# One more state's drive product on GpSimd, in one unit of a selective scan

## The chip, the cores and the metric

The kernel runs on one core of a Trainium2 chip. The metric is the device time of one execution in microseconds (us), as the median of several runs. TensorE does matrix products, VectorE elementwise work and the scans, ScalarE activations, GpSimd elementwise work on SBUF alone and the scatters, SyncE issues DMAs.

## The reference, cut to what matters

One layer: a Mamba block (selective scan) with residual, then a mixture of eight experts, on x of shape 4 x 32 x 32 x 64, that is four batches of 1024 tokens. In the block 128 channels carry 16 states each:

```
def step(h, inp):
    u_t, d_t, B_t, C_t = inp
    dA = exp(d_t[..., None] * A)
    h = dA * h + (d_t * u_t)[..., None] * B_t[:, None, :]
    y = einsum('bdn,bn->bd', h, C_t)
```

For each state n the kernel therefore needs a decay, exp(delta * A[n]), a drive, (delta * u) * B[n], the scan over the tokens, and the product of h with C[n], which is summed over the states.

## The kernel before, in words

Channels lie on the 128 partitions and tokens along the free dimension, so one state of one batch is a tile of 128 x 1024. The work is cut into five units: three whole batches (units 0, 1 and 2), the first 768 tokens of the fourth (unit 3, CARRY) and its last 256 (unit 4, LAST). Every engine has its program written out by hand; the engines meet only through semaphores, and each takes its instructions in program order. For units 0 to 3 each engine loops over n = 0..15.

For one state n of unit v, with k = 16 v + n:

- SyncE loads row n of B into the tile bsb (L398) and of C into csb (L405), each broadcast over the partitions, in rings of four. The load of a B row waits until the drive four states back is counted in s_mul, that of a C row until the product four states back is counted in s_pP. Both are in one queue, in the order C(n), B(n+2).
- ScalarE writes the decay to dA (L697, `decay`), a ring of three, two states ahead.
- VectorE multiplies delta * u, which lies in the PSUM tile Cp, by the row of B into the PSUM tile Bp (L1277, `drive`), and then scans dA and Bp into h (L1318, `scan`). The drive of the next state follows each scan, since Bp holds one state.
- GpSimd multiplies h by the row of C into prod (L518, `scan` of that engine), and TensorE adds prod to Yp (L984).

A state in the list POOLED goes another way. GpSimd makes its drive in place in bsb (L567, `drive` of that engine) from te, the SBUF copy of delta * u, two states ahead in its loop. VectorE skips L1277 for it. Since Bp is then free, ScalarE writes the decay of that state into Bp (L707, `decay_pooled`), in two halves of 512 tokens: the first once the first half of the scan of state n-1 has been made, the second once that scan is whole. So the scans of n-1 and of n are both cut in two (SPLIT), and each half scan of n waits for its half of the decay. The list holds states 2 and 5 of units 1, 2 and 3. The counts s_dA and s_mul of a pooled state are added with those of the next state.

Beside its states each unit's loop carries the `front` of the next batch (projections, delta, delta * u) and the `back` of the unit before (norms, routing, rows for the scatter), piece by piece: front(f, n) and back(v, n) are the pieces with number n. ScalarE's loop for one n is, in this order:

```
if n + 2 < 16 and (v, n + 2) not in POOLED:
    decay(v, n + 2)
if (v, n + 1) in POOLED:
    decay_pooled(v, n + 1)
```

then back (for n under 8) and front(v+1, n). Its front has at n = 4 two table loads around the silus, at n = 5 and 6 the two halves of what delta is made of (L665 and L666, each half behind a "step" matmul L963 on TensorE), at n = 6 also the exponential of it (L669), and at n = 7 its logarithm (L672, L674). TensorE's loop at n = 6 has the 8 product pairs L1024 of back, which wait for ScalarE's copy bT (L748), ahead of L963. GpSimd's front has at n = 7 a sum that waits for that exponential (L526), and at 9, 12 and 13 three more products; VectorE's front has at n = 11 a COPY_PREDICATED (L1270; batch 0 has its own at L1440), and its back has at n = 8 the residual add L1343.

After the units come the routed rows: scatters to a table in DRAM (L558), the expert stage on TensorE (L1142, L1153, L1167) and the scatter of the result.

Of the kernel before, what the change touches and what calls it, by code (L numbers as in the profile page):

```python
# [38 lines left out]
LAST, CARRY = V - 1, V - 2  # L39
NOWHERE = 1 << 20  # L40
CSLOTS = 4
POOLED = [(v, n) for v in range(1, LAST) for n in (2, 5)]
SPLIT = [(v, n + i) for v, n in POOLED for i in (-1, 0)]


# [17 lines left out]
def metaformer_layer(nc, x, ln_g, ln_b, in_proj_w, conv_w, conv_b, x_proj_w, dt_proj_w, dt_proj_b, A_log,  # L63
# [7 lines left out]
    with ExitStack() as ctx:  # L71
# [179 lines left out]
        def at(buf, b):  # L251

            return buf[:, b % 2, :]
# [112 lines left out]
        def _(sp):  # L366
# [52 lines left out]
            for v in range(LAST):  # L419
# [3 lines left out]
                for n in range(N):  # L423
# [9 lines left out]
                    if v == CARRY and n == 7:  # L433
                        sp.wait_ge(p_bx, len(POOLED))
                    if v == CARRY and n == 4:
# [23 lines left out]
        def _(pool):  # L459
# [60 lines left out]
            def front(f, n):  # L520
                if n == 9:
                    pool.wait_ge(f_ln, f + 1)
                    po.tensor_tensor(tabs[:, :], yt_free[:, :], tabs[:, :], ALU.subtract).then_inc(f_less, 1)
                if n == 7:
                    pool.wait_ge(f_exp, f + 2)
                    po.tensor_tensor(trel[:, :], trel[:, :], ex[:, :], ALU.add).then_inc(f_high, 1)  # L526
                if n == 12:
                    pool.wait_ge(f_pick, f + 1)
                    pool.wait_ge(f_high, f + 1)
                    if f >= 2:  # L530
                        pool.wait_ge(s_dA, N * (f - 1))
                    po.tensor_tensor(at(delta, f), trel[:, :], tabs[:, :], ALU.subtract).then_inc(f_delta, 1)
                if n == 13:
                    pool.wait_ge(f_delta, f + 1)
                    po.tensor_tensor(te[:, :], at(delta, f), at(u, f), ALU.mult).then_inc(f_dus, 1)
# [26 lines left out]
            def drive(v, n):  # L562
                k, c = N * v + n, span(v)
                pool.wait_ge(f_dus, UNITS[v][0])
                pool.wait_ge(b_in[k % CSLOTS], 16 * (k // CSLOTS + 1))
                row = bsb[:, k % CSLOTS, c]
                po.tensor_tensor(row, te[:, c], row, ALU.mult).then_inc(p_bx, 1)  # L567

            last_slot = po.to_reg(E * CAP - 1)
            for v in range(LAST):  # L570
                for n in range(16):
# [4 lines left out]
                    if v + 1 < B:  # L576
                        front(v + 1, n)
                    if (v, n + 2) in POOLED:
                        drive(v, n + 2)
# [43 lines left out]
        def _(act):  # L623
# [5 lines left out]
            def front(f, n):  # L629
# [45 lines left out]
                if n == 8:  # L675
                    ac.activation(yt_free[:, :], yt_free[:, :], ACT.Copy, bias=-1.0).then_inc(f_ln, 1)
                    act.wait_ge(p_bx, sum(x < f for x, _ in POOLED))
                    ac.activation(te[:, :], ex[:, :], ACT.Square, scale=0.5 ** 0.5)
# [14 lines left out]
            def decay(v, n):  # L693
                k, c = N * v + n, span(v)
                if k >= 3:
                    act.wait_ge(s_scan, k - 2)
                ac.activation(dA[:, k % 3, c], at(delta, UNITS[v][0])[:, c], ACT.Exp,  # L697
                              scale=aneg[:, n:n + 1]).then_inc(s_dA, 2 if (v, n - 1) in POOLED else 1)

# [135 lines left out]
            for v in range(LAST):  # L835
# [5 lines left out]
                for n in range(16):  # L841
                    if n + 2 < 16 and (v, n + 2) not in POOLED:
                        decay(v, n + 2)
# [717 lines left out]
```

## Time and profile before

| | us |
|---|---|
| median of 3 runs | 388.14 |
| lowest and highest run | 387.02, 391.14 |
| span of the profiled execution | 397.8 |
| VectorE busy in it | 310.1 (78%) |
| TensorE busy | 316.1 (79%) |
| GpSimd busy | 282.1 (71%) |
| ScalarE busy | 233.3 (59%) |

The span goes from the first instruction to the last one of one execution under the profiler. The page gives no other time of that execution; the runs are timed without it. Busy shares are averages over stages with different limits. Unit 1 lies at about 100 to 162 us.

### The profile page before, as it was taken

The numbers are of one execution on the slowest core, as the hardware profiler recorded it, in microseconds if no ns is written. First come the engines' busy times: TensorE is split into PE (matmuls) and PEld (weight loads), VectorE is DVE, ScalarE is ACT, GpSimd is POOL, SyncE is SP. The second block draws the span as 40 slices with busy tenths as digits, with TensorE's granted clock in tenths as the row PEclk, the third lists the DMA queues.
The fourth block names the chain that finished last, engine by engine and source line by source line (L and its number), as shares of the span: only waits on it lengthen the run. The fifth ranks groups of instructions, "written<-read, shape, count | busy, mean of one in ns | idle before, by whom it ended". The sixth has DMA issues, their size and how long they took to land. (4 is left out here: it accounts for less than half of the span.)

```text
span 397.8 us, 4347 instructions
## 1 busy us (share of the span) xinstructions
PE 316.1 (79%) x1257; PEld 188.4 (47%) x1257; DVE 310.1 (78%) x360; ACT 233.3 (59%) x519; POOL 282.1 (71%) x201
## 2 busy tenths in 40 slices
PE   7832986957989896897989698796895798869784
PEld 3311432313535352553545265363773576748764
DVE  4799987999999999987999989999981157425441
ACT  4456797524798984659797268775651455234221
POOL 3435846987993999999599999966877044745760
PEclk9965897999998998879899898989987599968955
DMA  4287999999798699856878769997210900000000
GB/s 99 36 281 248 274 243 366 390 200 368 315 315 323 208 308 297 284 190 244 303 254 298 203 175 325 318 369 226 61 30 19 250 23 4 18 8 17 16 1 8
DMA packets 43986, 78.68 MB, mean 198 GB/s; under 512 B 16050, under 2 KB 26093, under 8 KB 43962
## 3 DMA queue, kind: packets, MB, share of 16 engines
q1 hardware_dynamic: 41066, 73.88, 57.5%
q0 software_dynamic: 2896, 4.53, 4.2%
q8 instruction: 10, 0.16, 0.2%
q14 instruction: 14, 0.11, 0.1%
HBM read 72.30 MB, written 7.54 MB: 201 GB/s over the span
## 5 line engine op out<-in xcount | busy, mean ns | idle before, releaser
L518 POOL TENSOR_TENSOR prod<-h,csb 128x1024 f32<-128x1024 f32 (+1 forms) x64 | 143.7, 2253 | 24.9 <-DMA csb<-bc_rows 10.5
L984 PE MATMUL Yp<-prod,ident 128*128 128x512 f32 (+1 forms) x256 | 124.9, 624 | 13.8 <-POOL prod L518 13.6
L1318 DVE TENSOR_TENSOR_SCAN h<-dA,Bp 128x1024 f32<-128x1024 f32 (+2 forms) x58 | 119.7, 2064 | 4.7 <-DVE Bp L1277 1.0
L984 PEld LDWEIGHTS Yp<-prod,ident 128*128 128x128 f32 x256 | 50.3, 208 | 75.3 <-issue 50.3
L697 ACT ACTIVATE dA<-delta,aneg 128x1024 f32<-128x1024 f32 (+1 forms) x58 | 62.9, 1093 | 23.1 <-DVE h L1318 19.0
L1277 DVE TENSOR_TENSOR Bp<-Cp,bsb 128x1024 f32<-128x1024 f32 (+1 forms) x58 | 67.7, 1168 | 6.4 <-DMA bsb<-bc_rows 4.2
L615 POOL DMA_INDIRECT out_dram<-dA,csb x30 | 30.3, 1009 | 36.5 <-DVE dA L1509 28.9
L558 POOL DMA_INDIRECT slots<-rows_,slot x30 | 30.1, 1002 | 6.9 <-issue 4.5
L1495 DVE TENSOR_TENSOR dA<-Bp,b2s 128x320 f32<-128x320 f32 (+1 forms) x8 | 3.8, 475 | 33.8 <-PE Bp L1167 15.6
L1153 PE MATMUL Cp<-prod,w1s 128*128 128x384 f32 (+1 forms) x64 | 24.7, 508 | 2.0 <-issue 2.0
L895 ACT ACTIVATE bsb<-Yp,b1c 128x256 f32<-128x256 f32 x16 | 7.6, 475 | 23.4 <-PE Yp L1184 14.0
L1167 PEld LDWEIGHTS Bp<-w2s,prod 128*128 128x128 f32 x152 | 18.5, 195 | 2.3 <-issue 1.0
L1167 PE MATMUL Bp<-w2s,prod 128*128 128x64 f32 x152 | 18.3, 276 | 0.2 <-ACT prod L888 0.2
L1196 PEld LDWEIGHTS M<-w2s,bsb 128*128 128x128 f32 x64 | 13.6, 269 | 7.3 <-issue 5.7
L1196 PE MATMUL M<-w2s,bsb 128*128 128x64 f32 x64 | 12.9, 344 | 4.8 <-issue 4.8
L1153 PEld LDWEIGHTS Cp<-prod,w1s 128*128 128x128 f32 x64 | 12.1, 216 | 7.4 <-issue 5.4
L878 ACT ACTIVATE prod<-Bp 64x384 f32<-64x384 f32 (+1 forms) x16 | 6.8, 427 | 14.8 <-PE Bp L1142 7.6
L1184 PE MATMUL Yp<-hxT,w1s 72*128 72x256 f32 x32 | 13.7, 519 | 0.6 <-issue 0.6
L567 POOL TENSOR_TENSOR bsb<-te,bsb 128x1024 f32<-128x1024 f32 (+1 forms) x6 | 13.1, 2179 | 1.2 <-DMA bsb<-bc_rows 1.1
L615 POOL DMA_INDIRECT out_dram<-dA,bsb x10 | 10.1, 1013 | 4.7 <-issue 2.9
L526 POOL TENSOR_TENSOR trel<-trel,ex 128x1024 f32<-128x1024 f32 x3 | 7.1, 2359 | 8.7 <-DVE h L1318 4.9
L886 ACT ACTIVATE prod<-Cp,b1c 128x384 f32<-128x384 f32 (+1 forms) x16 | 8.4, 525 | 7.9 <-PE Cp L1153 5.8
(290 smaller groups left out, 604.8 us busy)
## 6 DMA issues: line engine op xcount, KB each, us to landing
bsb<-bc_rows SPq DMA_DIRECT2D x48, 512.0 KB, 6.7
csb<-bc_rows SPq DMA_DIRECT2D x48, 512.0 KB
bsb<-bc_rows SPq DMA_DIRECT2D x16, 384.0 KB, 5.7
csb<-bc_rows SPq DMA_DIRECT2D x16, 384.0 KB
slots<-fill POOLq DMA_DIRECT2D x1, 2600.0 KB
csb<-slots SPq DMA_DIRECT2D x6, 325.0 KB, 5.3
bcs<-bc_rows SPq DMA_DIRECT2D x2, 512.0 KB, 10.9
xs_in<-in_x_dram SPq DMA_DIRECT2D x1, 768.0 KB, 5.8
```

The costliest lines, as they stand in the source:

```text
L518: po.tensor_tensor(prod[:, k % 4, c], h[:, k % 3, c], csb[:, k % CSLOTS, c], ALU.mult).then_inc(s_pP, 1)
L558: po.indirect_dma_start(slots_dram[:, :], bass.IndirectOffsetOnAxis(ap=slot[:, v % 2, t:t + 1], axis=0), rows(v)[:, t, :], None, bounds_ch ...
L567: po.tensor_tensor(row, te[:, c], row, ALU.mult).then_inc(p_bx, 1)
L615: po.indirect_dma_start(out_rows, bass.IndirectOffsetOnAxis(ap=xe[e][:, k, R_ID:R_ID + 1].bitcast(I32), axis=0), yo[:, e % 2, k, :], None, ...
L697: ac.activation(dA[:, k % 3, c], at(delta, UNITS[v][0])[:, c], ACT.Exp, scale=aneg[:, n:n + 1]).then_inc(s_dA, 2 if (v, n - 1) in POOLED e ...
L984: ins = te_.matmul(Yp[:, c], idn, prod[:, k % 4, c], start=False, stop=(n == 15), skip_group_check=True)
L1153: te_.matmul(Cp[:, k * HALF:k * HALF + (k1 - k0) * P], w1s[:, e, k * P:(k + 1) * P], xT[:, e % 2, k0 * P:k1 * P], start=True, stop=True).t ...
L1167: ins = te_.matmul(turned_down(i)[:, (k - k0) * C:(k - k0 + 1) * C], part[:, e % 2, k * P:(k + 1) * P], w2s[:, e, x, :], start=(x == 0), s ...
L1184: te_.matmul(Yp[:, j % 2 * HALF:j % 2 * HALF + LW], w1s[0:HX, e, part * P:(part + 1) * P], hxT[0:HX, :], start=True, stop=True).then_inc(d ...
L1196: ins = te_.matmul(M0[:, t * C:(t + 1) * C], hid[:, j % 2, t * P:(t + 1) * P], w2s[:, e, part, :], start=False, stop=(j == BLOCKS - 1 and ...
L1277: ve.tensor_tensor(Bp[:, span(v)], Cp[:, span(v)], bsb[:, k % CSLOTS, span(v)], ALU.mult).then_inc(s_mul, 2 if (v, n - 1) in POOLED else 1)
L1318: ins = ve.tensor_tensor_scan(h[:, k % 3, c], decays, drives, h[:, k % 3, c.start - 1:c.start] if i else 0.0, ALU.mult, ALU.add)
```

## The change

State 8 of unit 1 joins the list POOLED. Its drive is then made by GpSimd ahead of its product of state 6, its decay goes to Bp in two halves, and the scans of states 7 and 8 of unit 1 are cut in two. Everything else follows from the list: in unit 1 the decay of state 8 is no longer issued at n = 6 of ScalarE's loop, its two halves are issued at n = 7, behind the decay of state 9, and VectorE's drive of state 9 counts for two.

```
-POOLED = [(v, n) for v in range(1, LAST) for n in (2, 5)]
+POOLED = [(v, n) for v in range(1, LAST) for n in ((2, 5, 8) if v == 1 else (2, 5))]
 SPLIT = [(v, n + i) for v, n in POOLED for i in (-1, 0)]
```

## Rows read from the trace of the kernel before

**Rows 1.** The page: its first line, and one line of its DMA issues.

```profile
span 397.8 us, 4347 instructions
...
bsb<-bc_rows SPq DMA_DIRECT2D x48, 512.0 KB, 6.7
```

**Rows 2.** The chain that ended last, its first piece kept: start, length, what.

```profile
280.11 1.30 DVE h L1297 x2
```

**Rows 3.** Busy time in stretches: start:end length, each engine, clock, DMA.

```profile
125.00:165.00 40.00, 33.65 (x114) 15.97 (x112) 38.84 (x37) 28.75 (x58) 35.88 (x17) 0.96 0.86 286
...
230.00:280.00 50.00, 40.91 (x193) 26.02 (x192) 46.29 (x53) 35.27 (x109) 40.92 (x31) 0.93 0.86 280
```

**Rows 4.** Timeline of VectorE, unit 2, the scan of state 5.

```profile
181.22 1.22 DVE L1318 TENSOR_TENSOR_SCAN h<-Bp,bsb 128x512 f32<-128x512 f32 x1 [3.37 <-ACT Bp L707]
...
183.93 1.23 DVE L1277 TENSOR_TENSOR Bp<-Cp,bsb 128x1024 f32<-128x1024 f32 x1
```

**Rows 5.** Timeline of VectorE, unit 1, states 4 to 9: start, length, instruction.

```profile
112.15 1.22 DVE L1318 TENSOR_TENSOR_SCAN h<-dA,Bp 128x512 f32<-128x512 f32 x1
...
114.60 1.20 DVE L1318 TENSOR_TENSOR_SCAN h<-Bp,bsb 128x512 f32<-128x512 f32 x1
...
118.60 2.29 DVE L1318 TENSOR_TENSOR_SCAN h<-dA,Bp 128x1024 f32<-128x1024 f32 x1
...
122.25 2.29 DVE L1318 TENSOR_TENSOR_SCAN h<-dA,Bp 128x1024 f32<-128x1024 f32 x1
124.56 1.23 DVE L1277 TENSOR_TENSOR Bp<-Cp,bsb 128x1024 f32<-128x1024 f32 x1
125.89 2.29 DVE L1318 TENSOR_TENSOR_SCAN h<-dA,Bp 128x1024 f32<-128x1024 f32 x1
128.21 1.23 DVE L1277 TENSOR_TENSOR Bp<-Cp,bsb 128x1024 f32<-128x1024 f32 x1
```

**Rows 6.** Timeline of TensorE ahead of the second half of front(2,6).

```profile
122.92 1.90 PE L1024 MATMUL M<-PW,bT 65*128 65x64 f32 x16
124.65 1.08 PE L963 MATMUL M<-u,wdt 128*128 128x512 f32 x2
```

**Rows 7.** Timeline of ScalarE, unit 1; in brackets the idle time before, and its end.

```profile
121.80 0.57 ACT L748 ACTIVATE bT<-M 65x512 f32<-65x512 f32 x1
...
123.42 1.14 ACT L697 ACTIVATE dA<-delta,aneg 128x1024 f32<-128x1024 f32 x1
125.76 0.69 ACT L665 ACTIVATE tabs<-M,dtb 128x512 f32<-128x512 f32 x1 [1.20 <-PE M L963]
...
128.07 1.13 ACT L697 ACTIVATE dA<-delta,aneg 128x1024 f32<-128x1024 f32 x1
```

**Rows 8.** Timeline of ScalarE, unit 2, before the half decays of state 5.

```profile
174.10 0.22 ACT L733 ACTIVATE sq<-M 128x64 f32<-128x64 f32 x1 [4.54 <-PE M L1006]
...
179.38 1.14 ACT L697 ACTIVATE dA<-delta,aneg 128x1024 f32<-128x1024 f32 x1
180.42 1.29 ACT L707 ACTIVATE Bp<-delta,aneg 128x512 f32<-128x512 f32 x2
```

**Rows 9.** Timeline of GpSimd, unit 1, products 5 and 6 and front at n = 7.

```profile
117.32 2.36 POOL L518 TENSOR_TENSOR prod<-h,csb 128x1024 f32<-128x1024 f32 x1 [0.15 <-DVE h L1318]
121.02 2.36 POOL L518 TENSOR_TENSOR prod<-h,csb 128x1024 f32<-128x1024 f32 x1 [1.34 <-issue]
128.24 2.37 POOL L526 TENSOR_TENSOR trel<-trel,ex 128x1024 f32<-128x1024 f32 x1 [4.86 <-DVE h L1318]
```

**Rows 10.** Timeline of SyncE's queue, the load of B's row 8 of unit 1.

```profile
112.09 0.32 SPq L398 DMA_DIRECT2D bsb<-bc_rows  x1
```

**Rows 11.** Timeline of VectorE, the two predicated copies, batch 0's and unit 1's.

```profile
26.33 1.29 DVE L1440 COPY_PREDICATED tabs<-small,te 128x1024 f32<-128x1024 uint8 x1
...
140.68 2.68 DVE L1270 COPY_PREDICATED tabs<-small,te 128x1024 f32<-128x1024 uint8 x1
```

**Rows 12.** Busy time in one stretch of unit 2; columns as in the third group.

```profile
168.00:170.00 2.00, 2.00 (x6) 1.31 (x6) 1.89 (x2) 1.55 (x2) 2.00 (x1) 0.50 0.69 263
```

## What the change should do to the time

> **What bounds the kernel now.** I read four views, in this order. The page gives the span of the profiled execution, 397.8 us [rows 1]. The chain that ended last is kept only from 280.11 us on [rows 2]; it begins with a VectorE scan of the last unit and goes on through TensorE's expert stage, so it says where the end hangs on VectorE, and nothing of the stretch that is changed. For that I cut the span into stretches: in 125 to 165 us VectorE is busy 38.84 of 40.00 us, against 35.88 on GpSimd and 28.75 on ScalarE; in 230 to 280 it is 46.29 of 50.00 [rows 3]. The gaps that are left there are mostly the 0.1 us between dependent instructions. So from the second batch's unit (unit 1, about 100 to 162 us) to the chain's first piece, VectorE's own order of instructions sets the time, and what it loses or wins in unit 1 arrives at the end unless a later wait takes it up. The only longer wait is one of 3.37 us in unit 2 for ScalarE's half decay, L707 [rows 4]. It is of the very kind that the change makes a third of, so its cause counts.
>
> The last view is the timeline of each engine over states 4 to 9 of unit 1. The reader is to see in it that an idle engine (GpSimd before L526) has room, and that a ScalarE that shows busy and waiting pieces in turn still decides when its next piece can come, since it takes its work in program order.
>
> **What the change takes from VectorE.** State 8's product (L1277, 1.23 us) goes, and the scans of states 7 and 8 are cut in two halves each, as those of states 4 and 5 are now. An uncut pair with both products goes from the scan of state 6 at 118.60 to that of state 8 at 125.89, 7.29 us; the cut pair from 112.15 to 118.60, 6.45 us [rows 5]. If nothing is late the change saves 7.29 - 6.45 = 0.84 us.
>
> **What it asks of ScalarE.** State 8's decay is no longer written to dA ahead of time. It goes into the PSUM tile Bp in two halves, the first after the first half scan of state 7. In ScalarE's order it stands elsewhere too: decay(8) was issued at n=6, before front(2,6); the two halves come at n=7, behind front(2,6) and decay(9). Front(2,6) can't start early. It waits for the second "step" matmul L963, which TensorE runs at 124.65 for 1.08 us, behind L1024 (122.92, 1.90 us) [rows 6]; L1024 itself waits for the copy bT at 121.80 [rows 7]. ScalarE gets to front(2,6) at 125.76 after 1.20 us of idling; without decay(8) (123.42, 1.14 us) it idles longer and starts at the same 125.76. decay(9) starts at 128.07 [rows 7], and its own condition, the end of scan 6, was met at 120.89. These times don't move, so the working is:
> - decay(9) at 128.07. From a decay to the half decay behind it is 180.42 - 179.38 = 1.04 us in unit 2 [rows 8]: first half at 129.11.
> - From there to the half scan that waits for it is 181.22 - 180.42 = 0.80 us [rows 4, 8]: state 8's scan starts at 129.91. VectorE has finished state 7 at 122.25 + 2.45 = 124.70 (two half scans take 2.45 us from 112.15 to the next at 114.60 [rows 5]). That is a stall of 5.2 us, and nothing else is in VectorE's order between the two.
> - From that half scan to the next product is 183.93 - 181.22 = 2.71 us [rows 4]: the product of state 9 starts at 132.62, against 128.21 now [rows 5]. The lateness is **4.4 us** (5.2 of stall less 0.84 saved, within rounding).
>
> Behind the wait VectorE has the residual add L1343 and then everything else of unit 1, which is its dense stretch. ScalarE's own later work slips far less: front(2,7) stands behind the two halves, which take 1.29 us together in unit 2 [rows 8], and VectorE, later by 4.4, doesn't wait for it.
>
> Bounds of this term: if L1024 starts as soon as the bT copy ends (121.80 + 0.57 = 122.37 instead of 122.92), all comes 0.55 us earlier, 3.9 us; if L963 ran at half clock, its 1.08 us doubled, 5.5 us. I take 4.4, the value of the rows themselves.
>
> **What it asks of GpSimd and the queues.** GpSimd gets one more product before product 6. Two of its instructions set end to end are 2.3 to 2.4 us apart, so it would run from about 119.7 to 122.0, behind product 5 (117.32, 2.36), and product 6 moves from 121.02 to 122.0, 1 us. The cover is the 4.86 us that GpSimd waits before L526 at 128.24 [rows 9], a wait that the row puts down to a scan long done; by the code it ends with front(2,6)'s exponential, done just before decay(9), and so stays. With product 6 done by 124.4 all is as before: cost nothing. Without that cover it would be 2.4 us on GpSimd, and VectorE would see them only after the two states by which a scan may run ahead of products. The new product needs row 8 of B, issued at 112.09 [rows 10]; a load takes 6.7 us to land [rows 1], so 118.8 and a little, just in time. Its result is wanted only at 129.9: 7.9 us to spare.
>
> On SyncE's queue the row of state 12 waits for the product of state 9, since that increment now stands for two: 132.6 + 1.23 = 133.9. Behind it stand the C rows of 11 and later. Product 7 sets the first of these (near 132.9, as now), so C row 11 is issued about 134.3, lands near 141, and is wanted by product 11 at about 144, since scans are later by 4.4. B row 12 lands near 141 too, its product comes near 144. Cost nothing, with some 3 us to spare.
>
> COPY_PREDICATED in unit 1 (L1270) meets GpSimd in another phase. It takes 2.68 us there and 1.29 at the start, where GpSimd stands still [rows 11]. Ends: 1.29 (-1.4 us) and 1.29 behind a whole product of 2.36, 3.65 (+1.0); I take no change, since a product lies beside it in both kernels. The Trainium skill's page "SBUF — State Buffer", section "Who interferes with whom", says that a VectorE instruction with two SBUF inputs and a GpSimd one that reads SBUF block each other for a whole instruction; the trace agrees, 2.68 against 1.29. By that rule the copy, which I work out to begin about 1.1 us into product 11, would wait out the other 1.25 and take 2.5 in all, and the sum would be 4.3 in place of 4.4.
>
> A scan isn't stretched by GpSimd's products: that at 125.89, with GpSimd idle, is followed by its next product after 2.32 us, that at 122.25, partly under product 6, after 2.31 [rows 5, 9]. Were scan 6 held by the new product after all, by 2.4 us at most, state 7's scan would still end before the half decay is written: nothing.
>
> **The sum.** 4.4 us on the way to the end of unit 1. Unit 2's start is a chain that VectorE sets off (yt, TensorE's projection, ScalarE's squares after a wait of 4.54 us, then the half decays [rows 8]), so it moves along. Units 2 and 3 are dense, and the expert stage follows the last rows. 397.8 [rows 1] becomes 402.2 in a profile. The timed median, 388.14, is 9.7 us under the span; I take that gap as untouched and add the same 4.4 us to the median: 392.5, 1.1% slower. A measurement of this kernel can tell about 1% (3.9 us) from no change, since its three runs lie 4.1 us apart.
>
> **Rivals.**
> - *The change does what it says*: the half decay is there when VectorE wants it, and 0.84 us are saved: 387.3. It decides by whether ScalarE writes the first half by 124.7. It speaks for it that five of the six cut pairs now go through without such a wait. Against it: in those the half decay doesn't stand behind a wait for TensorE, and here it would have to come 5.2 us earlier than the order allows. 0.06.
> - *The loss is given back in unit 2.* The 3.37 us stall there came with TensorE at a granted clock of 0.50, that is at 1.2 GHz, in all of 168 to 170 us [rows 12], inside the chain that leads to it. If the later schedule leaves it at 2.4 GHz there, the stall goes and 4.4 - 3.4 = 1.0 remains: 389.2. For it: TensorE's work and pauses ahead of it are moved. Against: they come in the same order. 0.20.
> - *More than the sum*: TensorE, which waits longer in unit 1, meets the half clock where ScalarE hangs on it, in L1024 and L963 (twice 1.90 and 1.08 is 3.0 us more at most) or at the start of unit 3, where the pair at state 5 has no room either. 4.4 + 1.1 to 4.4 + 3.0: 393.6 to 395.5. 0.14.
>
> **How the numbers follow.** My forecast has 0.60: 392.5, by its bounds 391.5 to 393.6. The range takes in the second rival and most of the third, and leaves out the first and the far end of the third, about 0.12, and some for the spread of the medians: 389.0 to 394.6. The bound for slower, 392.0, lies just under my forecast: of its 0.60 I put 0.41 above, with the third rival's 0.14 that is 0.55. Faster by over 1% is in none of the cases by itself; 0.02 for spread. Within 1%: the remaining 0.43.
>
> **What would show it.** In the changed profile: a wait of about 5 us of VectorE before state 8's first half scan, ended by ScalarE L707; ScalarE's two halves right behind decay(9); GpSimd's seven L567 with the new one near 120 us and its wait before L526 still there, shorter at its start; COPY_PREDICATED between 1.3 and 3.7 us; unit 2's stall again near 3.4. I am wrong if that wait is under 2 us, if the half decays stand before front(2,6), or if unit 2's stall is gone.

## The result, and the profile after

The changed kernel is slower. Its first four runs have a median of 394.99 us (391.56 to 399.54), four runs of the kernel before beside them one of 387.58 (384.58 to 391.14); the ratio is 1.0158, 95% interval 1.0098 to 1.0218, that is 3.8 to 8.5 us. A second measurement, six runs against 23, gave 392.69 and 1.0181 (1.0123 to 1.0238).

VectorE's timeline in unit 1 of the changed kernel, against [rows 5]; in brackets the idle time before, and its end:

```profile
118.80 2.29 DVE L1318 TENSOR_TENSOR_SCAN h<-dA,Bp 128x1024 f32<-128x1024 f32 x1
...
122.44 1.22 DVE L1318 TENSOR_TENSOR_SCAN h<-dA,Bp 128x512 f32<-128x512 f32 x1
123.69 1.28 DVE L1318 TENSOR_TENSOR_SCAN h<-dA,h,Bp 128x512 f32<-128x512 f32 x1
130.10 1.22 DVE L1318 TENSOR_TENSOR_SCAN h<-Bp,bsb 128x512 f32<-128x512 f32 x1 [5.13 <-ACT Bp L707]
...
132.81 1.23 DVE L1277 TENSOR_TENSOR Bp<-Cp,bsb 128x1024 f32<-128x1024 f32 x1
```

State 8's first half scan waits 5.13 us for ScalarE's half decay. From the scan of state 6 to the product of state 9 it is 132.81 - 118.80 = 14.01 us, against 128.21 - 118.60 = 9.61 before: 4.40 us lost. ScalarE's timeline shows why, against [rows 7]:

```profile
125.95 0.69 ACT L665 ACTIVATE tabs<-M,dtb 128x512 f32<-128x512 f32 x1 [2.24 <-PE M L963]
...
128.26 1.13 ACT L697 ACTIVATE dA<-delta,aneg 128x1024 f32<-128x1024 f32 x1
129.30 1.28 ACT L707 ACTIVATE Bp<-delta,aneg 128x512 f32<-128x512 f32 x2
```

Without decay(8) in its way ScalarE idles 2.24 us where it idled 1.20, and gets to front(2,6) no earlier, 7.15 us behind the start of scan 6 against 7.16. The half decays follow it and decay(9).

GpSimd's timeline, against [rows 9]: the new product runs from 120.03, product 6 comes 1.1 us later against product 5 than before, and 3.74 of the 4.86 us of waiting before L526 are left.

```profile
117.52 2.36 POOL L518 TENSOR_TENSOR prod<-h,csb 128x1024 f32<-128x1024 f32 x1 [0.16 <-issue]
120.03 2.35 POOL L567 TENSOR_TENSOR bsb<-te,bsb 128x1024 f32<-128x1024 f32 x1 [0.16 <-DMA bsb<-bc_rows]
122.34 2.35 POOL L518 TENSOR_TENSOR prod<-h,csb 128x1024 f32<-128x1024 f32 x1
128.43 2.35 POOL L526 TENSOR_TENSOR trel<-trel,ex 128x1024 f32<-128x1024 f32 x1 [3.74 <-ACT ex L669]
```

Further on, VectorE of the changed kernel at four points of units 2 to 4, and then the same of the kernel before but for the first, which is in [rows 4]:

```profile
182.35 1.20 DVE L1318 TENSOR_TENSOR_SCAN h<-Bp,bsb 128x512 f32<-128x512 f32 x1
...
208.43 5.17 DVE L1270 COPY_PREDICATED tabs<-small,te 128x1024 f32<-128x1024 uint8 x1
...
234.81 1.23 DVE L1333 TENSOR_TENSOR yt<-Yp,sz 128x1024 f32<-128x1024 f32 x1 [1.63 <-PE Yp L984]
...
281.10 1.23 DVE L1284 TENSOR_TENSOR Bp<-Cp,trel 128x1024 f32<-128x1024 f32 x1
```

```profile
207.33 3.13 DVE L1270 COPY_PREDICATED tabs<-small,te 128x1024 f32<-128x1024 uint8 x1
...
230.55 1.23 DVE L1333 TENSOR_TENSOR yt<-Yp,sz 128x1024 f32<-128x1024 f32 x1 [0.51 <-PE Yp L984]
...
276.55 1.23 DVE L1284 TENSOR_TENSOR Bp<-Cp,trel 128x1024 f32<-128x1024 f32 x1
```

The stall of 3.37 us at state 5 of unit 2 [rows 4] is gone here. TensorE's granted clock (the last number but two of these rows) was 1.00, that is 2.4 GHz, in the chain ahead of it at 170 to 176 us, where the kernel before had 0.53, mostly 1.2 GHz, at 166 to 172:

```profile
170.00:176.00 6.00, 6.00 (x37) 4.50 (x37) 5.77 (x5) 3.90 (x13) 5.02 (x4) 1.00 0.54 184
```

```profile
166.00:172.00 6.00, 6.00 (x24) 4.81 (x23) 5.68 (x6) 2.71 (x4) 5.17 (x5) 0.53 0.47 159
```

But the gain didn't last. COPY_PREDICATED of unit 2 took 5.17 us where it took 3.13, and yt (L1333) at the start of unit 3 waited 1.63 us for TensorE where it waited 0.51. At the first product of unit 4 the lateness is 281.10 - 276.55 = 4.55 us, 4.35 without the 0.20 by which unit 1 had begun later. The second profile of the changed kernel shows the same three: 5.13, 5.14 and 1.49 us.

**The clock between runs.** Nearly every run has its mean granted TensorE clock on record, and the time goes with it: the kernel before ran from 384.51 us at 0.897 to 391.47 at 0.864 in that second group. At 0.905 to 0.906 the kernel before took 386.34 to 386.62 us there (five runs), the changed one 391.23 (one run); at 0.869 it is 391.32 against 395.43 and 396.26. The distance at a like clock is thus 4 to 5 us. A line through the 176 runs of this study that have a clock on record, with one slope for the clock and one offset for each kernel, has 1.53 us for each 0.01, and these offsets from the kernel before (95%, in us; the scatter around the line is 1.4; the kernels are described in the next section):

| kernel | runs | ratio to the runs beside it | offset at a like clock |
|---|---|---|---|
| changed kernel | 10 | 1.0158, 1.0181 | +5.4 ± 0.9 |
| product of state 8 on VectorE | 6 | 1.0179 (1.0122 to 1.0236) | +4.5 ± 1.2 |
| copy apart from products | 10 | 1.0053 (1.0011 to 1.0095) | +3.2 ± 1.0 |
| early half decays | 12 | 1.0085 (1.0045 to 1.0125) | +1.7 ± 0.9 |
| extra GpSimd product alone | 12 | 1.0066 (1.0029 to 1.0104) | +0.7 ± 0.9 |
| two units | 12 | 1.0017 (0.9967 to 1.0067) | -0.9 ± 0.9 |
| early, product 7 first | 12 | 0.9970 (0.9915 to 1.0024) | -1.0 ± 0.9 |
| all cures | 12 | 0.9987 (0.9944 to 1.0029) | -1.3 ± 0.9 |
| GpSimd's cures without state 8 | 12 | 0.9977 (0.9929 to 1.0026) | -1.7 ± 0.9 |

The ratios go by the runs within 1.5% of the fastest of their kernel, the medians and the line by all runs; a line through the former alone puts the offsets up to 0.9 us elsewhere, the extra product's at +1.4 ± 0.9. The offsets describe; a kernel may also change how often the clock falls, and that part is then not in its offset.

### The profile page after: what moved, and what is told of

It is laid out like the page before. It is cut to its first block and busy times, and to the rows that moved or that the text cites. A ratio compares the mean times of both kernels' runs of the same rounds, so it can differ in the third digit from the quotient of the medians.

```text
span 392.4 us, 4352 instructions
## 1 busy us (share of the span) xinstructions
PE 306.9 (78%) x1257; PEld 181.5 (46%) x1257; DVE 310.8 (79%) x361; ACT 233.9 (60%) x520; POOL 282.2 (72%) x202
## 5 line engine op out<-in xcount | busy, mean ns | idle before, releaser
L518 POOL TENSOR_TENSOR prod<-h,csb 128x1024 f32<-128x1024 f32 (+1 forms) x64 | 141.9, 2221 | 32.3 <-DVE h L1318 11.6
L984 PE MATMUL Yp<-prod,ident 128*128 128x512 f32 (+1 forms) x256 | 129.4, 645 | 12.5 <-POOL prod L518 12.5
L1318 DVE TENSOR_TENSOR_SCAN h<-dA,Bp 128x1024 f32<-128x1024 f32 (+2 forms) x57 | 116.4, 2041 | 5.0 <-DVE Bp L1277 1.7
L984 PEld LDWEIGHTS Yp<-prod,ident 128*128 128x128 f32 x256 | 52.0, 214 | 74.7 <-issue 53.1
L1153 PE MATMUL Cp<-prod,w1s 128*128 128x384 f32 (+1 forms) x64 | 21.6, 462 | 0.0
L567 POOL TENSOR_TENSOR bsb<-te,bsb 128x1024 f32<-128x1024 f32 (+1 forms) x7 | 15.4, 2207 | 0.3 <-DMA bsb<-bc_rows 0.2
L707 ACT ACTIVATE Bp<-delta,aneg 128x512 f32<-128x512 f32 (+1 forms) x14 | 9.1, 657 | 7.9 <-DVE h L1318 7.6
L1318 DVE TENSOR_TENSOR_SCAN h<-Bp,bsb 128x512 f32<-128x512 f32 x7 | 8.5, 1209 | 5.3 <-ACT Bp L707 5.1
L1208 PE MATMUL Yp<-h,ident 128*128 128x256 f32 x32 | 10.1, 464 | 1.9 <-POOL h L591 1.9
L691 ACT ACTIVATE Cp<-te 128x1024 f32<-128x1024 f32 x3 | 3.1, 1029 | 14.0 <-DVE Bp L1277 14.0
```

What stands on the lines that cost most here:

```text
L518: po.tensor_tensor(prod[:, k % 4, c], h[:, k % 3, c], csb[:, k % CSLOTS, c], ALU.mult).then_inc(s_pP, 1)
L707: ac.activation(Bp[:, c], at(delta, UNITS[v][0])[:, c], ACT.Exp, scale=aneg[:, n:n + 1]).then_inc(p_dA, 1)
L984: ins = te_.matmul(Yp[:, c], idn, prod[:, k % 4, c], start=False, stop=(n == 15), skip_group_check=True)
L1153: te_.matmul(Cp[:, k * HALF:k * HALF + (k1 - k0) * P], w1s[:, e, k * P:(k + 1) * P], xT[:, e % 2, k0 * P:k1 * P], start=True, stop=True).t ...
L1208: ins = te_.matmul(Yp[:, c], idn, h[:, ring(p // 2), (p % 2 * 2 + i) * LW:(p % 2 * 2 + i + 1) * LW], start=False, stop=(p == 7 and i == 1) ...
L1318: ins = ve.tensor_tensor_scan(h[:, k % 3, c], decays, drives, h[:, k % 3, c.start - 1:c.start] if i else 0.0, ALU.mult, ALU.add)
```

## The experiments

**Early half decays.** The changed kernel with this in ScalarE's loop, for (1, 8) alone:

```
+EARLY = [(1, 8)]
...
-                    if n + 2 < 16 and (v, n + 2) not in POOLED:
+                    if n + 2 < 16 and (v, n + 2) not in POOLED and (v, n + 1) not in EARLY:
                         decay(v, n + 2)
-                    if (v, n + 1) in POOLED:
+                    if (v, n + 1) in POOLED and (v, n + 1) not in EARLY:
                         decay_pooled(v, n + 1)
+                    if (v, n + 2) in EARLY:
+                        decay_pooled(v, n + 2)
+                        decay(v, n + 3)
```

> The changed kernel, but in unit 1 ScalarE issues the two half decays of state 8, and then decay(9), at n=6 ahead of front(2,6) instead of behind it; GpSimd's third product, the cut scans and all else stay. Theory (the place of the half decays in ScalarE's order): VectorE's wait of 5.13 us before state 8's scan falls under 0.3 us, the product of state 9 starts 0.8 us earlier than in the kernel before, front(2,6) starts about 0.8 us later; the time is that of the kernel before, ratio 0.985 to 1.005. Rival (GpSimd's added product, or its use of SBUF beside VectorE, costs the time): it is still made, so the ratio stays at 1.010 to 1.020. Rival (cutting the scans costs more than it saves): the product of state 9 starts later than before though there is no wait.

Ratio 1.0085 (1.0045 to 1.0125), offset +1.7 us: most of the loss is gone, not all, and the ratio is over the 1.005 expected. VectorE's timeline (the file's lines lie four further down, so L1322 is the scan and L1281 the product):

```profile
123.59 1.28 DVE L1322 TENSOR_TENSOR_SCAN h<-dA,h,Bp 128x512 f32<-128x512 f32 x1
124.78 1.20 DVE L1322 TENSOR_TENSOR_SCAN h<-Bp,bsb 128x512 f32<-128x512 f32 x1
...
127.46 1.23 DVE L1281 TENSOR_TENSOR Bp<-Cp,bsb 128x1024 f32<-128x1024 f32 x1
...
131.51 1.23 DVE L1281 TENSOR_TENSOR Bp<-Cp,bsb 128x1024 f32<-128x1024 f32 x1
133.74 2.29 DVE L1322 TENSOR_TENSOR_SCAN h<-dA,Bp 128x1024 f32<-128x1024 f32 x1 [0.99 <-POOL prod L519]
```

State 8 no longer waits, as expected. But the scan of state 10 waits 0.99 us for GpSimd's product 7, and that stands behind L526 (here L527) in GpSimd's order:

```profile
122.36 2.35 POOL L519 TENSOR_TENSOR prod<-h,csb 128x1024 f32<-128x1024 f32 x1
129.03 2.36 POOL L527 TENSOR_TENSOR trel<-trel,ex 128x1024 f32<-128x1024 f32 x1 [4.32 <-ACT ex L670]
131.35 4.69 POOL L519 TENSOR_TENSOR prod<-h,csb 128x1024 f32<-128x1024 f32 x2
```

So a second wait lay hidden behind the first: GpSimd idles 4.32 us for an exponential, with the scan for product 7 already made.

**The changed kernel again**, without an edit, as the yardstick.

> The changed kernel itself again, as the yardstick of this group. Theory: 4.4 us, ratio 1.011; with the first measurement's 1.0158 in the interval. VectorE waits about 5.1 us before state 8's first half scan in this profile too, whatever the end of the kernel does. If the excess over 4.4 us is real and not scatter, the ratio comes out at 1.015 or more with an interval that leaves out 1.011.

1.0181, with 1.011 just outside; at a like clock +5.4 us, one more than my 4.4. The wait is 5.13 us again.

**The product of state 8 on VectorE.** GpSimd makes two products in unit 1, ScalarE's order is the changed one:

```
-                    if (v, n + 2) in POOLED:
+                    if (v, n + 2) in POOLED and (v, n + 2) != (1, 8):
                         drive(v, n + 2)
...
+                if (v, n + 1) == (1, 8):
+                    k = N * v + n + 1
+                    dve.wait_ge(b_in[k % CSLOTS], 16 * (k // CSLOTS + 1))
+                    row = bsb[:, k % CSLOTS, span(v)]
+                    ve.tensor_tensor(row, Cp[:, span(v)], row, ALU.mult).then_inc(p_bx, 1)
```

> The changed kernel, but VectorE makes the drive of state 8 itself, in place in bsb, behind the cut scan of state 7; GpSimd makes two products in unit 1 as before. The half decays stay behind front(2,6). Theory (ScalarE's order): VectorE does the 1.2 us product inside its wait, which shrinks from 5.1 to about 3.8 us and ends at the same point; the product of state 9 starts where it does in the changed kernel, and the time is the changed kernel's, ratio 1.008 to 1.018. Rival (GpSimd's added product costs the time): the product is gone, so the ratio falls to 0.995 to 1.005.

Ratio 1.0179, as slow as the changed kernel. Its timeline of VectorE:

```profile
125.04 1.20 DVE L1327 TENSOR_TENSOR bsb<-Cp,bsb 128x1024 f32<-128x1024 f32 x1
130.25 1.22 DVE L1318 TENSOR_TENSOR_SCAN h<-Bp,bsb 128x512 f32<-128x512 f32 x1 [4.01 <-ACT Bp L707]
```

The product that the change took off VectorE fits into VectorE's wait, which shrinks to 4.01 us and ends where it did. Whether GpSimd or VectorE makes it doesn't matter while ScalarE is late.

**The extra GpSimd product alone**, in the kernel before:

```
+                    if (v, n) == (1, 6):
+                        po.tensor_tensor(extra[:, :], te[:, :], te[:, :], ALU.mult).then_inc(x_done, 1)
                     scan(v, n)
```

with a wait of ScalarE for x_done before it writes te again.

> The kernel before with one more GpSimd product of the same size at the same place (te times te into a tile that nothing reads, ahead of product 6 of unit 1); state 8 keeps VectorE's product and the decay in dA. Theory: product 6 starts 1 us later, GpSimd's wait before L526 shrinks from 4.9 to 3.7 us, VectorE shows no new wait, ratio 0.995 to 1.005. Rival (GpSimd's added product costs the time): ratio 1.006 to 1.020, and VectorE's scans or products beside it last longer or wait for GpSimd.

By its ratio, 1.0066, it missed: the interval leaves out no change. At a like clock the offset is +0.7 ± 0.9 us. Its one run at 0.905 took 386.39 us, where five of the kernel before took 386.34 to 386.62; six of its twelve runs lay under a clock of 0.875, and six of the 23 beside it. So the ratio is at least in part a matter of which clock its runs met; whether the extra product has a part in that, or a cost of its own, stays open. In the profile no scan or product of VectorE in states 6 to 9 waits, and GpSimd still waits 4.39 us before L526 (here L528). The extra product was shorter than the true one, 1.89 us:

```profile
121.86 1.89 POOL L583 TENSOR_TENSOR extra<-te 128x1024 f32<-128x1024 f32 x1
...
130.47 2.37 POOL L528 TENSOR_TENSOR trel<-trel,ex 128x1024 f32<-128x1024 f32 x1 [4.39 <-DVE h L1324]
```

**Half the dose.** The changed kernel with the half decays of state 8 ahead of decay(9), still behind front(2,6):

```
+                    if (v, n + 1) == (1, 8):
+                        decay_pooled(v, n + 1)
                     if n + 2 < 16 and (v, n + 2) not in POOLED:
                         decay(v, n + 2)
-                    if (v, n + 1) in POOLED:
+                    if (v, n + 1) in POOLED and (v, n + 1) != (1, 8):
                         decay_pooled(v, n + 1)
```

> The changed kernel, but ScalarE issues the two half decays of state 8 ahead of decay(9) and still behind front(2,6). A half dose: theory says that the first half starts where decay(9) did, 1.04 us earlier, so VectorE's wait falls from 5.13 to about 4.1 us and the product of state 9 starts 1.0 us earlier. A theory that puts the wait down to GpSimd's product or to its row of B expects no change of the wait.

```profile
129.25 1.22 DVE L1320 TENSOR_TENSOR_SCAN h<-Bp,bsb 128x512 f32<-128x512 f32 x1 [4.09 <-ACT Bp L707]
```

4.09 us: one decay less ahead of the halves, 1.04 us less of wait. It ran once (392.68 us), so its time says little.

**Product 7 first.** Early half decays, and in GpSimd's loop for n = 7 of unit 1:

```
-                    if v + 1 < B:
+                    if v + 1 < B and (v, n) != (1, 7):
                         front(v + 1, n)
                     if (v, n + 2) in POOLED:
                         drive(v, n + 2)
                     scan(v, n)
+                    if (v, n) == (1, 7):
+                        front(v + 1, n)
```

> The kernel with the early half decays, and in unit 1 GpSimd makes product 7 ahead of front(2,7) (L526) instead of behind it. Theory (with ScalarE on time, GpSimd's order is next in line): VectorE's wait of 0.99 us for product 7, before the scan of state 10, is gone, GpSimd's wait before L526 shrinks by about 2.3 us, and from unit 1's first product to the scan of state 10 VectorE is 0.8 us ahead of the kernel before. Ratio 0.992 to 1.006; among runs of like granted clock within 1 us of the kernel before. Rival (GpSimd has no room at all in this unit): the wait only moves to a later scan of unit 1 and stays near 1 us.

Ratio 0.9970 (0.9915 to 1.0024), offset -1.0 us; no scan of unit 1 behind state 8 waits for a product. GpSimd makes product 7 at 127.49 us now, and VectorE's scan of state 10 follows without a wait:

```profile
127.49 2.36 POOL L519 TENSOR_TENSOR prod<-h,csb 128x1024 f32<-128x1024 f32 x1 [0.62 <-issue]
```

```profile
135.32 2.29 DVE L1324 TENSOR_TENSOR_SCAN h<-dA,Bp 128x1024 f32<-128x1024 f32 x1
```

In this profile a stall of 3.18 us at state 5, ahead of all this, had put VectorE later against GpSimd; the kernel with all cures, whose unit 1 had no stall, shows the same without it.

**The copy apart from products.** The changed kernel, with GpSimd waiting for COPY_PREDICATED one state sooner:

```
+                if n == 11:
+                    pool.wait_ge(f_pick, f + 1)
                 if n == 12:
                     pool.wait_ge(f_pick, f + 1)
```

> The changed kernel, but GpSimd waits for COPY_PREDICATED (L1270) ahead of product 11 instead of behind it, in every unit. Theory (the copy is held up by GpSimd's products, and back to back products can take the shared way twice): the copy never meets two products, so its 5.17 us of unit 2 fall to 3.65 or less; unit 1's 2.5 us stay between 1.3 and 3.7. VectorE's wait of 5.1 us before state 8's scan stays. Ratio 1.008 to 1.018, at most 2 us under the changed kernel. Rival (the 5.17 us have nothing to do with GpSimd, but come from the copy's inputs): the copy of unit 2 still takes about 5 us where VectorE reaches it early.

```profile
149.05 1.30 DVE L1272 COPY_PREDICATED tabs<-small,te 128x1024 f32<-128x1024 uint8 x1
...
211.03 2.84 DVE L1272 COPY_PREDICATED tabs<-small,te 128x1024 f32<-128x1024 uint8 x1
```

1.30 us with GpSimd waiting beside it, as at the start [rows 11], and 2.84 behind a product. Ratio 1.0053 (expected 1.008 to 1.018), offset +3.2 us, 2.2 under the changed kernel (2.0 at most expected), with VectorE's wait at state 8 still there (5.54 us).

**All cures**: the last two edits and the early half decays together.

> Both cures together: early half decays, product 7 ahead of L526, and GpSimd waiting for COPY_PREDICATED ahead of product 11. Theory: VectorE has no wait in unit 1, the copies take 1.3 to 2.6 us where they took 2.7 to 3.3, and the time is 0.5 to 2.5 us under the kernel before at a like granted clock; ratio 0.990 to 1.003. Rival (GpSimd becomes late by waiting): VectorE's scans of states 13 to 15 wait for products, and the time is over that of the kernel before.

VectorE's timeline of unit 1 (L1326 is the scan, L1285 the product, L1278 the copy):

```profile
118.32 2.29 DVE L1326 TENSOR_TENSOR_SCAN h<-dA,Bp 128x1024 f32<-128x1024 f32 x1
...
124.42 1.20 DVE L1326 TENSOR_TENSOR_SCAN h<-Bp,bsb 128x512 f32<-128x512 f32 x1
...
127.10 1.23 DVE L1285 TENSOR_TENSOR Bp<-Cp,bsb 128x1024 f32<-128x1024 f32 x1
...
132.47 2.29 DVE L1326 TENSOR_TENSOR_SCAN h<-dA,Bp 128x1024 f32<-128x1024 f32 x1
...
139.57 1.99 DVE L1278 COPY_PREDICATED tabs<-small,te 128x1024 f32<-128x1024 uint8 x1
```

Nothing waits from state 6 to the copy. From the scan of state 6 to the product of state 9 it is 8.78 us, against 9.61 in [rows 5]: 0.83 saved. The copies took 1.99 us here and 2.79 in unit 2, the latter over the 2.6 expected. The time is 386.46 against 388.37 beside it, ratio 0.9987, offset -1.3 us.

**GpSimd's cures without state 8**: product 7 first and the copy apart, in the kernel before.

> The kernel before with GpSimd's two changes of order alone: product 7 of unit 1 ahead of L526, and the wait for COPY_PREDICATED ahead of product 11; two products per unit as before. It tells what of the time of the kernel with all cures is owed to the third state. Theory: the copies cost 0.5 to 1.5 us less in all, so the time is 0.5 to 1.5 us under the kernel before at a like clock, ratio 0.994 to 1.002, and the kernel with the third state on top is 0.8 us under this one. Rival (the third state is worth nothing even when nothing is late): this kernel is as fast as that one.

Offset -1.7 us, ratio 0.9977. It isn't slower than the kernel with all cures; 0.84 us between the two is less than these runs tell: they ran in different groups, on different chips, and with an offset for each group as well the line has -1.6 ± 1.0 for all cures and -1.1 ± 1.0 without state 8. That the third state pays in the time is thus not shown.

**Two units**: all cures, with state 8 pooled, its half decays early and product 7 first in unit 2 as well.

> The kernel with all cures, and state 8 pooled in unit 2 as well, with its half decays ahead of front(3,6) and product 7 ahead of L526 there too. Theory: no wait of VectorE before state 8 of unit 2, another 0.84 us saved there, ratio 0.990 to 1.001, 0.8 us under the kernel with one unit at a like clock. Rival (GpSimd, which also issues eight scatters in unit 2, has no room): VectorE waits for products in unit 2, and the time is 1 to 4 us over that kernel.

Offset -0.9 us: no gain from the second unit. VectorE, GpSimd and ScalarE in unit 2, one line of each:

```profile
190.79 1.22 DVE L1326 TENSOR_TENSOR_SCAN h<-Bp,bsb 128x512 f32<-128x512 f32 x1 [0.76 <-ACT Bp L712]
```

```profile
188.34 2.36 POOL L570 TENSOR_TENSOR bsb<-te,bsb 128x1024 f32<-128x1024 f32 x1
```

```profile
188.75 0.69 ACT L712 ACTIVATE Bp<-delta,aneg 128x512 f32<-128x512 f32 x1 [0.33 <-DVE h L1326]
```

The profile puts the 0.76 us down to ScalarE, whose first half had been done at 188.75 + 0.69 = 189.44. GpSimd's product ended at 190.70, and that is what the scan waited for: in unit 2 GpSimd also issues a scatter of 1.01 us in each of these states. The wait takes back nearly all of the 0.84 us. The rival for that unit was right in its mechanism, not in its price: it had 1 to 4 us over the kernel with all cures, and the offsets lie 0.4 us apart.

## Why the prediction was right, and where not

- **ScalarE's order** was the cause, and its working held to a tenth: a wait of 5.13 us for 5.2, a loss of 4.40 for 4.4. Moving the half decays ahead of front(2,6) took the wait away, moving them by one decay took 1.04 us of it, and taking the product off GpSimd again took nothing.
- **0.84 us saved** when nothing is late: 0.83 in the kernel with all cures. The rows show it; it is under what the times tell.
- **GpSimd's product at nothing** held in the rows: 3.74 us of cover were left in the changed kernel and 4.32 with the half decays early. In the times the extra product alone is +0.7 ± 0.9, which doesn't exclude a small cost. The 0.99 us that VectorE waited for product 7 with ScalarE on time, two states later as I had named, isn't the added product's: GpSimd idled 4.32 us ahead of L526, and product 7 stands behind that. In the kernel before, product 7 (the first of two in this row) was done at about 132.9 us, and the scan of state 10 began at 133.58:

```profile
130.56 4.70 POOL L518 TENSOR_TENSOR prod<-h,csb 128x1024 f32<-128x1024 f32 x2
```

```profile
133.58 2.29 DVE L1318 TENSOR_TENSOR_SCAN h<-dA,Bp 128x1024 f32<-128x1024 f32 x1
```

  That is 0.7 us of room. With the half decays early VectorE comes 0.8 us sooner and the exponential 0.7 us later, so the room is gone.
- **SyncE's queue** did as worked out: B row 12 was issued at 134.07 (133.9 forecast), C row 11 at 134.44 (134.3), and no one waited for either.

```profile
134.07 0.32 SPq L398 DMA_DIRECT2D bsb<-bc_rows  x1
134.44 0.43 SPq L405 DMA_DIRECT2D csb<-bc_rows  x1
```

- **COPY_PREDICATED** took 2.48 us in unit 1, 2.51 in the second profile:

```profile
145.29 2.48 DVE L1270 COPY_PREDICATED tabs<-small,te 128x1024 f32<-128x1024 uint8 x1
```

  The rule of the Trainium skill, page "SBUF — State Buffer", section "Who interferes with whom", that the later of two such instructions is blocked for the whole of the other, had given 2.5; the trace agrees in unit 1. In unit 2 the copy would by that rule have taken 3.0 us had it had the next turn, an estimate from the rows (1.67 us left of a product, then 1.29); it took 5.17, held up by two products. The step of the prediction that failed is the upper bound, "1.29 behind a whole product", and that I asked for it in unit 1 alone.
- **Unit 2's stall**, the second rival: it went, in both profiles of the changed kernel, and I had named that as a sign of being wrong. It stayed in those with the product on VectorE, 3.35, and with half the dose, 3.39. These came to unit 2 as late as the changed kernel (yt at 168.78 and 168.44 us against 168.69), but their granted clock was 0.50 in 174 to 176 us, where the changed kernel had 1.00. So the mechanism of the rival is there, but being late isn't enough for it, and what kept the clock up stays open. Its result isn't there: 4.40 - 3.37 + 2.04 (copy) + 1.12 (yt) = 4.2 us, against 4.35 measured. In this part the sum came out by luck: a gain of 3.37 us that the forecast didn't have was made up by 3.16 us of losses that it didn't have either. I had left out who would be met by a VectorE that comes early there.
- **The gap of 9.7 us** between span and median was misread. The changed kernel's profiled execution took 394.15 us with a span of 392.4, so 1.8 us lie around a span. The profile of the kernel before caught an execution with a long last stage; this row of it, in the expert stage, is far behind the change:

```profile
355.63 0.49 DVE L1495 TENSOR_TENSOR dA<-Bp,b2s 128x320 f32<-128x320 f32 x1 [10.84 <-remote]
```

  It did no harm, since I added a difference, but "402.2 in a profile" came out as 392.4.
- **The size.** 4.4 us lie inside 3.8 to 8.5; at a like clock it is 5.4 ± 0.9, a little more. The copy is a likely place, since keeping it apart from the products took 2.2 us off the changed kernel; how often it meets two products in runs without a profile wasn't seen, and so this stays argued. The end of the units is another. Here is yt of unit 4, first in the changed kernel, then in the kernel before:

```profile
308.25 0.42 DVE L1333 TENSOR_TENSOR yt<-Yp,sz 128x256 f32<-128x256 f32 x1 [2.98 <-PE Yp L1208]
```

```profile
302.08 0.42 DVE L1333 TENSOR_TENSOR yt<-Yp,sz 128x256 f32<-128x256 f32 x1 [2.98 <-PE Yp L1208]
```

  Less the 0.20 the lateness is 5.97 us there, where it was 4.35 at the first product of unit 4; in the second profile of the changed kernel yt comes at 305.68, 3.9 us late by the same count. So from one execution to the next the loss differs by 2 us before the expert stage begins.

## What to carry to other kernels

An instruction that is moved from "long ahead" to "just in time" has to be followed in the order of the engine that issues it: what stands in front of it there, and what that in turn waits for, is its price. When a wait of 5 us goes, look for the next one in the other engines' orders before counting the gain: here one cure in ScalarE's order needed another in GpSimd's. And where one kernel's runs differ by more than the effect, compare them at a like granted clock, or count from the rows of a stretch.

## What the runs showed of the hardware that was not expected

The predicated copy, with two inputs in SBUF, took 1.3 us with GpSimd still, 2 to 3.4 us beside one of its products, and twice 5.1 to 5.2 us. In that case three products of GpSimd ran back to back:

```profile
205.46 6.96 POOL L518 TENSOR_TENSOR prod<-h,csb 128x1024 f32<-128x1024 f32 x3
213.68 2.41 POOL L532 TENSOR_TENSOR delta<-trel,tabs 128x1024 f32<-128x1024 f32 x1 [1.25 <-DVE tabs L1270]
```

VectorE's copy was in line from 208.43, during the second product; the third began behind it at about 210.1 and yet ran first, to 212.4, and the copy took the 1.2 us from there to 213.6, in which GpSimd waited. So an instruction that is held up doesn't get the next turn for sure; what decides it, these runs don't show. In the kernel before, where the copy began at 207.33, it took 3.13 us, one product's worth.

Executions of one kernel on one chip (the kernel before, 23 runs) had mean granted clocks from 0.864 to 0.905 and times from 384.51 to 391.47 us: a spread of 7 us, more than any edit here is worth.
